# A decoder layer on one core: the denominators of the time mixing inverted in pairs, and the stages of every engine in another order

## What is computed

```python
x = _layernorm(x + _L0_attn_ref(x, ...))
x = _layernorm(x + _L0_xattn_ref(16, 128, 256, time_decay, time_first, x, ctx_2048))
x = _layernorm(x + _L0_ffn_ref(x, w1, w2, w3))

# _wkv, one step: k is x, v is ctx
y_t = (e1 * aa + e2 * vt) / (e1 * bb + e2)
aa, bb = e1b * aa + e2b * vt, e1b * bb + e2b
```

## Time and profile before

| what | value |
|---|---|
| median of 3 runs | 262.02 us |
| lowest and highest | 260.38 and 263.08 us |
| the profiled execution: its own time | 262.2 us |
| its span in the trace | 260.4 us |
| VectorE busy | 217.7 us (84%) |
| TensorE busy | 208.2 us (80%) |
| GpSimd busy | 161.5 us (62%) |
| ScalarE busy | 160.9 us (62%) |

### The profile page before, as it was taken

How to read it: one execution, slowest core, us unless ns; L and a number is a source line. 1 busy time by engine, 2 the same in 40 slices (tenths; PEclk the granted TensorE clock), 3 DMA queues, 4 the chain that set the end, 5 groups by cost and what they waited for, 6 DMA issues and landing times.

```text
span 260.4 us, 9989 instructions
## 1 busy us (share of the span) xinstructions
PE 208.2 (80%) x3778; PEld 139.9 (54%) x3778; DVE 217.7 (84%) x544; ACT 160.9 (62%) x329; POOL 161.5 (62%) x336
## 2 busy tenths in 40 slices
PE   1759699989899999999999999999997795625611
PEld 0235457657666666666666666766665662413310
DVE  2534987999999999999999999999999977686331
ACT  2212175446686877777777787777777665655631
POOL 0100007647866869696968778787777787876541
PEclk9986869999999999999999999999999757555665
DMA  6920002102020020212201120203020201000001
GB/s 194 369 66 23 3 1 65 58 7 64 4 64 3 3 83 23 65 29 58 61 26 43 44 71 17 84 3 83 5 63 3 63 3 40 10 13 21 0 20 42
DMA packets 11968, 12.34 MB, mean 47 GB/s; under 512 B 1872, under 2 KB 11152, under 8 KB 11920
## 3 DMA queue, kind: packets, MB, share of 16 engines
q1 hardware_dynamic: 11200, 11.67, 14.5%
q10 hardware_dynamic: 720, 0.03, 0.2%
HBM read 9.60 MB, written 2.10 MB: 45 GB/s over the span
## 4 chain that ended last, share of the span: by engine, by line
PE 50%; DVE 22%; issue 18%; ACT 4%; POOL 3%; DMA 1%; DVEq 1%; POOLq 0%; ACTq 0%
PE ps_qkv L393 13%; PE ps_s L429 9%; PE ps_o L476 5%; PE ps_w L379 4%; DVE amax_h L972 4%; PE ps_c L528 4%; DVE vT L863 3%; PE ps_a L514 3%; DVE qkD L858 3%; PE ps_b L514 3%; DVE gate L965 2%; DVE den_rec L941 2%; PE ps_o L379 2%; DVE wsum L1009 2%; PE ps_o L462 2%
## 5 line engine op out<-in xcount | busy, mean ns | idle before, releaser
L393 PE MATMUL ps_qkv<-wqkv,xT 128*128 128x512 f32 x64 | 35.5, 683 | 1.9 <-DVE qkv_tok L842 1.9
L733 POOL TENSOR_TENSOR var_eps<-mv,eps 128x1 f32<-128x1 f32 x48 | 9.2, 192 | 39.8 <-DVE mv L925 39.3
L745 POOL TENSOR_TENSOR hid<-gate,up_s 128x352 f32<-128x352 f32 x32 | 29.8, 932 | 2.1 <-ACT up_s L628 1.8
L736 POOL TENSOR_TENSOR rstd<-var_eps,minus_half 128x1 f32<-128x1 f32 x48 | 26.4, 551 | 3.8
L941 DVE RECIPROCAL den_rec<-frac 128x256 f32<-128x256 f32 x16 | 27.7, 1733 | 0.0
L429 PE MATMUL ps_s<-qkD 20*64 20x64 f32 x1024 | 23.9, 234 | 3.3 <-PE ps_s L429 3.3
L462 PE MATMUL ps_o<-probs,v_blk 64*32 64x64 f32 x1024 | 21.7, 225 | 4.6 <-DVE res L908 3.6
L577 ACT ACTIVATE qkv_tok<-ps_qkv 128x512 f32<-128x512 f32 x16 | 9.6, 598 | 25.3 <-PE ps_qkv L393 25.3
L387 PE MATMUL ps_qkv<-wqkv,xT 128*128 128x256 f32 x64 | 19.8, 431 | 6.1 <-DMA wqkv<-wqkv_in 5.3
L429 PEld LDWEIGHTS ps_s<-qkD 20*64 20x64 f32 x1024 | 19.8, 143 | 8.1 <-PE ps_s L429 5.1
L660 ACT ACTIVATE hqT<-ps_c 128x768 bf16<-128x768 bf16 x16 | 13.0, 811 | 16.4 <-PE ps_c L521 16.4
(11 more groups left out here) (110 smaller groups left out, 569.5 us busy)
## 6 DMA issues: line engine op xcount, KB each, us to landing
xT<-xT_in SPq DMA_DIRECT2D x16, 128.0 KB, 2.4
x_res<-x_in SPq DMA_DIRECT2D x16, 128.0 KB, 2.7
ctxT<-ctxT_in SPq DMA_DIRECT2D x16, 128.0 KB, 2.4
out<-y_out SPq DMA_DIRECT2D x16, 128.0 KB, 1.7
w_raw<-w_in SPq DMA_DIRECT2D x2, 704.0 KB, 6.7
wqkv<-wqkv_in SPq DMA_DIRECT2D x2, 384.0 KB, 4.2
w_raw<-w_in SPq DMA_DIRECT2D x1, 640.0 KB, 8.6
wo<-wo_in SPq DMA_DIRECT2D x1, 256.0 KB, 4.9
```

Of the source, the lines that this page charges most:

```text
L393: last = mm(ps_kv, xT[k.slot][:, h, :], wqkv[:, h, C:3 * C], start=h == 0, stop=h == 1)
L736: g.tensor_tensor(rstd[i][:], var_eps[i][:], minus_half[:], ALU.pow).then_inc(rstd_done[i], 1)
L745: g.tensor_tensor(hid[:, half * FH:(half + 1) * FH], gate[half][:], up_s[half][:], ALU.mult).then_inc(hid_done[half], 1)
```

## The change

The quotients of two neighbouring steps share one inversion: with denominators a and b, the inverse of the product r = 1/(a*b) is taken, and the two quotients are n_a*b*r and n_b*a*r. GpSimd forms the 128 products of a partition (`pair_dens`), and two instructions of 128 elements each form the cross products (`cross_terms`). All their inputs, and the outputs of the cross products, are taken with a step of two elements. VectorE inverts 128 elements instead of 256. `divide` still has 256 elements; it now reads `cross` and each inverse twice. The bound on the exponents, `U_CUT`, goes from 60 to 50, so that products of two denominators stay in range.

In the same change the lists of stages of all engines are written in another order. The core of the diff; of the lists only GpSimd's is shown whole:

```diff
-U_CUT = 60.0
+U_CUT = 50.0
...
-        den_rec = sb("den_rec", [P, HALVES, P])
+        den_pair = sb("den_pair", [P, HALVES, P // 2])
+        cross = sb("cross", [P, HALVES, P])
+        den_rec = sb("den_rec", [P, HALVES, P // 2])
...
+            def pair_dens(k):
+
+                wait(pool, frac_done, k.t + 1)
+                wait(pool, den_recips, k.t)
+                g.tensor_tensor(den_pair[:], frac[:, 0, :, even], frac[:, 0, :, odd], ALU.mult).then_inc(pairs_done, 1)
+
+            def cross_terms(k):
+                wait(pool, frac_done, k.t + 1)
+                wait(pool, y_ready, k.t)
+                g.tensor_tensor(cross[:, :, even], frac[:, 1, :, even], frac[:, 0, :, odd], ALU.mult)
+                g.tensor_tensor(cross[:, :, odd], frac[:, 1, :, odd], frac[:, 0, :, even], ALU.mult).then_inc(crossed, 1)
+
             def divide(k):
-                wait(pool, frac_done, k.t + 1)
+                wait(pool, crossed, k.t + 1)
                 wait(pool, den_recips, k.t + 1)
                 wait(pool, y_turned, k.t)
-                g.tensor_tensor(yT[:], frac[:, 1], den_rec[:], ALU.mult).then_inc(y_ready, 1)
+                g.tensor_tensor(yT[:].rearrange("p h (n l) -> p (h n) l", l=2),
+                                cross[:].rearrange("p h (n l) -> p (h n) l", l=2),
+                                den_rec[:].rearrange("p h n -> p (h n)").unsqueeze(2).broadcast_to([P, C // 2, 2]),
+                                ALU.mult).then_inc(y_ready, 1)
...
             def step(at):
+                on(at(3), add_now)
                 on(at(5), hidden, 1)
-                on(at(3), weigh_past)
-                on(at(3), weigh_now)
+                on(at(3), pair_dens)
+                on(at(3), cross_terms)
                 on(at(4), whole_x)
-                on(at(3), add_now)
+                on(at(3), divide)
+                on(at(2), inv_std, 0)
+                on(at(6), inv_std, 2)
                 on(at(4), ffn_scales)
-                on(at(2), inv_std, 0)
+                once(at(2), ternary_weights)
                 on(at(5), whole_h)
-                once(at(2), ternary_weights)
-                on(at(3), divide)
+                on(at(3), inv_std, 1)
+                on(at(2), weigh_past)
+                on(at(2), weigh_now)
                 on(at(4), hidden, 0)
-                on(at(6), inv_std, 2)
-                on(at(3), inv_std, 1)
...
             def recip_den(k):
-                wait(dve, frac_done, k.t + 1)
+                wait(dve, pairs_done, k.t + 1)
                 wait(dve, y_ready, k.t)
-                v.reciprocal(den_rec[:], frac[:, 0]).then_inc(den_recips, 1)
+                v.reciprocal(den_rec[:], den_pair[:]).then_inc(den_recips, 1)
```

More of the change, by code:

```diff
@@ L536, in step @@
             def step(at):
[L537 to L540, removed]
                 on(at(5), turn_xq)
-                on(at(2), weigh_v, 0)
+                on(at(4), turn_y)
+                on(at(2), weigh_v, 1)
                 on(at(5), up, 0)
[L544 to L550, removed]
                 on(at(3), turn_k)
                 on(at(1), score)
+                on(at(6), turn_hq)
+                on(at(1), block_v)
+                on(at(5), up, 1)
                 on(at(2), turn_attn)
+                on(at(6), down)
+                on(at(0), project_q)
+                on(at(2), project_out)
+                once(at(2), sum_weights)
+                on(at(1), shift)
+                on(at(0), project_kv)
+                on(at(1), weigh_v, 0)
             run_steps(step)
@@ L666, in step @@
             def step(at):
[L667 to L668 removed]
+                on(at(3), exp_k)
+                on(at(5), copy_up, 0)
+                on(at(6), copy_hq)
+                on(at(1), copy_v_blocks)
+                on(at(5), tanh_gate, 1)
+                on(at(2), copy_attn)
+                on(at(5), copy_up, 1)
+                once(at(2), round_weights)
+                on(at(4), layernorm, 1)
                 on(at(1), exp_scores, 0)
                 on(at(1), exp_scores, 1)
+                on(at(4), scale_x)
+                on(at(0), copy_kv)
                 on(at(4), copy_xq)
[L672 removed]
+                on(at(2), layernorm, 0)
                 on(at(5), scale_h)
+                on(at(6), layernorm, 2)
                 on(at(4), tanh_gate, 0)
[L675 to L684, removed]
             run_steps(step)
@@ L1039, in step @@
-                on(at(1), max_hi_part)
-                on(at(4), recip_x)
-                once(at(2), cut_weights, 2)
-                on(at(1), max_lo_part)
-                on(at(3), scan)
-                on(at(0), turn_v)
-                on(at(5), amax_of_h)
-                on(at(2), residual, 0)
+                on(at(1), max_quads)
+                once(at(2), weight_scales)
+                on(at(1), max_rows)
+                on(at(1), max_hi_part)
+                on(at(3), scan)
+                on(at(1), max_lo_part)
@@ new lines, in step @@
+                on(at(5), gate_up, 1)
+                on(at(6), residual, 2)
+                on(at(6), moments, 2)
+                on(at(4), amax_of_x)
+                on(at(2), residual, 0)
+                on(at(0), copy_q)
+                on(at(4), floor_x)
+                on(at(2), moments, 0)
+                on(at(4), recip_x)
+                on(at(2), mean_var, 0)
+                on(at(3), recip_den)
+                once(at(2), cut_weights, 0)
+                once(at(2), cut_weights, 1)
@@ L1063, in step @@
                 on(at(5), scale_of_out)
                 on(at(1), normalise)
+                once(at(1), weight_sums)
+                once(at(0), wkv_tables)
             run_steps(step)
```

41 lines of the change are left out of this document (16 added, 25 removed).

## The result

The changed kernel has a median of 273.12 us (4 runs, 272.71 to 273.27), the kernel before beside it 262.55 us: a ratio of 1.042 (95% interval 1.035 to 1.048). It is slower, by more than twice what was forecast (266.0), and outside the range (259.0 to 272.0). The profiled execution took 273.05 us, its span is 271.3.

The account below looks back on a forecast made before the run. VectorE bound the kernel before at 12.37 us per step; GpSimd's row plus scan would make 12.65. From 262.2, -0.7 for three first periods and +4.3 for twelve others gave 265.8, stated as 266.0 us, range 259.0 to 272.0.

Parts of the forecast that it names:

- small waits in the row: GpSimd's row: whole_x waiting for ScalarE's scaled x, and VectorE's attn falling beside a normalisation; 0.15 us together, an estimate.
- rest of the scan: Part of VectorE's scan that cannot run beside GpSimd's last hidden, delaying add_now: 1.22 - 0.13 = 1.09 us.
- closed loop: GpSimd's add_now through its last hidden, then the scan's rest and 0.08 until a waiting instruction starts: 12.5 us per step.
- Its own signs of being wrong: Scan at 1.22 beside full-speed hidden; new instructions far from 0.46 us; period 12.0 with VectorE full; long wait elsewhere.
- I leave both at zero net: Filling up to the first inversion and draining after the last: no net change, 2 us each way.
- The three first periods: Start of the run, GpSimd's row not yet full: VectorE's 0.3 less per period counts, -0.7 us from 34.74.
- The unheld scan: Rival: the scan isn't held and VectorE sets a period of 12.0; 258.4 us, faster; chance 0.17.
- The meeting of the loops: Rival: small products take 0.30 us, small waits vanish, GpSimd's loop is 12.2; near 261.5 us; chance 0.20.
- the first rival: The unheld scan: nine undisturbed periods save 0.34 us each, the three first 0.7 together; chance 0.17.
- The inversion: Rival: VectorE's inversion stays at 1.73 us, VectorE needs 12.8 per step; near 267.5 us; chance 0.03.
- The price of the step of two: Rival: GpSimd's products with a two-element step cost like 256 elements, loop 13.45; 275.4 us; chance 0.10.

Follow-up runs that it names:

- cast_on_act: The changed kernel with the cast max_hi moved from VectorE to ScalarE; 271.54 us, 1.032 against the kernel before.
- third_x2: The changed kernel with a third buffer for x2, so layernorm 1 waits for an older residual; 269.72 us, 1.029 against the kernel before.
- x2_and_cast: The changed kernel with both a third buffer for x2 and the cast max_hi on ScalarE; 265.28 us, 1.013 against the kernel before.
- one_cross: The changed kernel without one of the two cross products, its lane filled with ones once; 275.74 us, 1.050 against the kernel before.
- divide_early: The kernel before with the products and shorter inversion, in the old order except divide moved ahead of whole_h on GpSimd; 281.53 us, 1.069.
- turn_y_first: The kernel of divide_early with turn_y also ahead of turn_hq in TensorE's list; 279.80 us, 1.069 against the kernel before.
- inv1_x2_cast: The kernel of x2_and_cast with inv_std 1 moved behind hidden 0 in GpSimd's list; 277.66 us, 1.060 against the kernel before.
- inv1_beside_scan: The changed kernel with inv_std 1 moved behind hidden 0 in GpSimd's list; 279.74 us, 1.066 against the kernel before.

## Why the prediction was wrong

**What was right.** The direction, and that the two engines hold each other: VectorE was the bound before; the inversion takes 0.93 us (0.94 forecast); the three products take 1.30 us from start to start (1.23 forecast: 0.36, 0.47, and 0.47); an instruction of the one engine holds the scan or the cast of the other until it ends, and GpSimd idles through the scan (1.24 us, forecast 1.17). By the Trainium skill (SBUF — State Buffer, SBUF: two separate sides), whichever of two instructions that need the shared port pair starts first has it for its whole length. The trace agrees, with a small difference: 0.21 of hidden's 0.93 us ran beside the scan in `cast_on_act`. The price of a step of two elements was no issue: 0.40 to 0.52 us lies near the 0.46 on the line between the rows. The Trainium skill (GPSIMD Engine Reference, Performance pitfalls for Q7 kernels) has a slower rate only for steps of more than 8 bytes; the trace shows no sign of one at 8.

**The step that failed in size.** "On top come small waits in the row ... I take 0.15 for both together." The wait at whole_x alone is 0.50 us from start to start. I had seen that it depends on "an inversion that VectorE now reaches some 4 us after the scan's start, just as GpSimd gets there", and priced a near tie at nearly nothing. It is 4.25 us (132.84 to 137.09), and what makes GpSimd wait is in those 4.25: 0.29 us in which amax_x waits for layernorm 1, and that for residual 2. This wait, between a write and an old read of a buffer, is in the code of `layernorm` and was not in my sum; `third_x2` prices it at 0.39 a step. GpSimd's row by terms, measured less forecast: products +0.07, whole_x's wait +0.35 (0.50 less the 0.15 for both small waits), whole_x and divide 0.00, the inv_std +0.07, ffn_scales +0.07, rest of the scan +0.07, all others -0.01. Together 0.62, and 13.26 instead of 12.64. With the two edits of `x2_and_cast` the period is 12.59 and the row nearly without gaps, close to the forecast's 12.65, though the limit is then VectorE's row with its held instruction as much as GpSimd's.

**The step that failed in kind.** "GpSimd's row (11.3 us) plus the scan that it may not overlap makes a closed loop": so the products would count in full. `one_cross` shows that they don't count at all: the loop of the changed kernel goes hidden, scan, residual 2, layernorm 1, amax_x, scaled x, whole_x, and the products lie beside it with 0.46 us to spare. So in the new order the pairs don't make the kernel slower: they save 0.86, about the 0.80 by which the inversion is shorter, since the long one would lie in the loop. In the old order they cost 0.52, and the order alone costs 1.75, more than the whole change. Nowhere in the prediction was the question put what each half of the change would do alone. Its own signs of being wrong fit: GpSimd is busy 10.88 us of 13.25 instead of over 11 in 12.5, and the long wait at ScalarE's scaled x is there.

**What else moved.** By the stretches of the earlier trace rows: up to the first inversion 48.83 (1.1 less), the first three periods 35.44 (forecast 34.0), the other twelve 157.1 (forecast 151.8; the last three are shorter than 13.26), the draining 29.9 (28.2). Of the 7.3 us between 265.8 and 273.05, the twelve periods are 5.3. "I leave both at zero net" for the ends was 0.6 too low, within its 2 us. The three first periods, forecast shorter by 0.7, came out longer by 0.7.

**The rivals.** The unheld scan (258.4) is refuted by the rows: a cast or a scan is held, or holds, in every run of the new order. The meeting of the loops (261.5) needed products of 0.30 us and no small waits; they took 1.30 for the three, and the wait was 0.50. Its own sum also gives 260.4 (twelve periods of 12.2, and 0.7 less in the first three), not 261.5; and the first rival's 0.34 saved in a period is 0.37 by its own 12.0. The inversion nearly halved, from 1.73 to 0.93 us. The price of the step of two (275.4) came nearest to the time, for a reason that wasn't so.

What stays open: which chain limits `divide_early` and `turn_y_first`; which of the reordered lists brings the 1.75 us, since no run has the new order on one engine alone; and whether an order exists in which a version with pairs beats the kernel before.

## What to carry to other kernels

Where VectorE and GpSimd take turns at the port, count their instructions as one row: an order that puts a long GpSimd instruction beside a VectorE one with two SBUF inputs, or beside a copy, makes one of them wait out the other in every period. When every engine has a little room, look for the loop through several engines and follow it across buffers too: a wait of a writer for an old reader (here two buffers of x2) turns a harmless order into a chain. And a change of two parts is to be priced part by part, and each part with and without the other: the time of the sum says nothing of the one that its name tells of, and a branch with 0.46 us to spare makes both its cost and its saving invisible.

## What the runs showed of the hardware

- A VectorE cast of 128x16 elements, 0.17 us by itself, took 0.96 to 0.98 us when it started with a GpSimd product of 352 elements. So it isn't only instructions with two inputs that are held. The reductions row_max (0.19) and quad_max (1.25) beside weigh_past and weigh_now of GpSimd were not lengthened.
- A GpSimd instruction of a single element, with two inputs, is held by VectorE's scan as a long one is: 1.11 us in `inv1_x2_cast` and 1.19 in `inv1_beside_scan`, instead of 0.19.
- GpSimd products of 128 fp32 elements with a step of two: 0.40 us where both inputs come from the same half of frac, 0.51 to 0.52 where they come from its two halves or the output has a step of two also; one run doesn't tell which of these it is.
- ScalarE took 0.51 us for rounding 256 elements and 0.88 for 704, where GpSimd needs 0.41 and 0.78.
